# Graph attention in three layers: the last stage run block by block inside layer 2's edge rounds

## The reference, cut to what matters

```
h    = x @ W_lin + b_lin
feat = h @ W_gat                                   # 8 heads of 32
e    = leaky_relu(el[src] + er[dst], 0.2)          # el, er: feat times two vectors
a    = softmax of e over the edges of one dst
out  = sum over edges of feat[src] * a + gat_bias
out  = leaky_relu(out, 0.01)
x    = layernorm(x + h + out)                      # the result
```

## Time and profile before

| | us |
|---|---|
| median of 3 runs | 6509.73 |
| lowest and highest run | 6506.02 and 6517.36 |
| span of the profiled execution | 6515.9 |
| of it from the last product of layer 2 to the end | 154 |

### The profile page before, as it was taken

The page is one execution under the profiler, slowest core; times in us unless marked ns, Lnnn a source line. Parts: engine busy times, 40 slices in busy tenths (PEclk is TensorE's granted clock), DMA queues, the critical chain, the costliest instruction groups (busy, mean ns, idle before and its releaser), DMA issues. The chain is left out here.

```text
span 6515.9 us, 110173 instructions
## 1 busy us (share of the span) xinstructions
PE 4981.0 (76%) x21652; PEld 3682.0 (57%) x21653; DVE 5313.4 (82%) x16735; ACT 2717.7 (42%) x4351; POOL 4585.1 (70%) x4837
## 2 busy tenths in 40 slices
PE   6788888888888577777777777758778778787876
PEld 5555655555556355555555555536656556566653
DVE  6788888888888788888888888877778778777788
ACT  3333333333333245554545455533333333333335
POOL 2777777777776577776767676737777777777764
PEclk8777877877777678777777777767777777778786
DMA  8555555555555455555555555535555555555545
GB/s 274 149 156 156 157 157 155 157 156 156 156 155 141 117 162 160 160 159 156 159 158 162 153 162 157 162 102 161 160 158 161 160 159 161 160 160 160 160 131 159
DMA packets 505894, 1027.11 MB, mean 158 GB/s; under 512 B 146891, under 2 KB 313199, under 8 KB 504878
## 3 DMA queue, kind: packets, MB, share of 16 engines
q0 software_dynamic: 226208, 633.50, 36.2%
q1 hardware_dynamic: 278798, 382.44, 18.1%
HBM read 931.37 MB, written 84.15 MB: 156 GB/s over the span
## 5 line engine op out<-in xcount | busy, mean ns | idle before, releaser
L1032 POOL DMA_INDIRECT e_rows<-table,loaded x4689 | 4489.2, 957 | 1756.8 <-issue 1392.6
L1266 PE MATMUL e_p_mm<-e_rows,e_onehot 128*128 128x264 f32 x9378 | 2466.5, 417 | 0.0
L1266 PEld LDWEIGHTS e_p_mm<-e_rows,e_onehot 128*128 128x128 f32 x9378 | 1876.3, 208 | 360.5 <-issue 20.1
L1444 DVE TENSOR_TENSOR e_rows<-e_rows,e_p_pair 128x1024 f32<-128x1024 f32 x1173 | 1417.8, 1209 | 0.0
L1436 DVE TENSOR_TENSOR e_onehot<-e_col,e_p_pair 128x512 f32<-128x512 f32 (+1 forms) x1467 | 953.4, 650 | 328.2 <-issue 280.4
L1259 PE MATMUL e_p_mm<-e_xmsg,e_onehot 128*128 128x264 f32 x1764 | 875.3, 669 | 103.3 <-ACT e_p_mm L1133 86.2
L1274 PE MATMUL e_p_one<-ad_parts,e_onehotT 128*128 x5586 | 707.8, 188 | 149.6 <-issue 143.3
L1225 ACT ACTIVATE e_rows<-e_gap 128x64 f32<-128x64 f32 (+1 forms) x294 | 80.6, 274 | 1621.0 <-DVE e_gap L1766 1614.7
L1274 PEld LDWEIGHTS e_p_one<-ad_parts,e_onehotT 128*128 128x128 bf16 x5586 | 550.4, 102 | 330.4 <-issue 193.3
L1139 ACT ACTIVATE e_onehotT<-e_onehotT,minus_pidx 128x2432 bf16<-128x2432 bf16 x294 | 681.0, 2316 | 42.0 <-DMA e_pass<-pass_rows 42.0
L1142 ACT ACTIVATE e_onehotT<-e_onehotT,one_col 128x2432 bf16<-128x2432 bf16 x294 | 682.6, 2322 | 9.6
(11 more groups left out here) (326 smaller groups left out, 5819.3 us busy)
## 6 DMA issues: line engine op xcount, KB each, us to landing
e_onehotT<-rel_rows SPq DMA_DIRECT2D x294, 608.0 KB
e_rows<-table,loaded POOLq DMA_INDIRECT x4689
e_own_row<-table SPq DMA_DIRECT2D x196, 128.0 KB
table<-e_rows_out SPq DMA_DIRECT2D x98, 132.0 KB
table<-n_rows_out SPq DMA_DIRECT2D x14, 910.0 KB, 15.6
table<-e_rows_out SPq DMA_DIRECT2D x98, 130.0 KB
n_inputs<-in_x_turned SPq DMA_DIRECT2D x14, 896.0 KB, 11.2
e_mask<-mask_rows SPq DMA_DIRECT2D x196, 64.0 KB
```

Of the source, the lines that this page charges most:

```text
L1032: pool.indirect_dma_start(rows[k][:, g, 0:TW], None, table[L], bass.IndirectOffsetOnAxis(ap=idx[k][:, g:g + 1], axis=0)).then_inc(s_gat[k] ...
L1266: ins = nc.tensor.matmul(p_mm[:, bass.ds(region, MW)], onehot[:, g, :], rows[k][:, g, :], start=False, stop=True, skip_group_check=True)
L1444: return nc.vector.tensor_tensor(feats, feats, p_e[:, gs, :].unsqueeze(3).to_broadcast([P, n, H, C]), ALU.mult)
```

## The change

`final_phase`, the array `resid` and `add_linear` are gone. In their place layer 2's rounds call `last_blocks` on SP and VectorE, `last_sums` on TensorE, and `inverse_roots`, `above_zero` and `last_rows` on ScalarE. Round w makes the share of place w - 4, the sums of place w - 5 and the scaled rows of place w - 6, and SP stores place w - 9 in its own round w. `summed` and `mv` have two buffers, `vin` and `turned` one. The two sums of a block, one for the part above zero and one with the residual and the slope 0.01, stand in the two halves of one PSUM bank. The inverse root is exp(-0.5 ln(var + eps)). After the last round the loops go on to drain the last blocks. Layer 2 now writes out 12 rounds, and no semaphores are cleared behind it.

```diff
 # SP, in round w, ahead of its wait for the look-up of round w - 2
+def last_blocks(w, u, i):
+    r, other = u % TURNS, (u + 1) % TURNS
+    if finished(w, 6):
+        if finished(w, 7):
+            wait_apart(sp, s["mm"], place_of(sp, w, 7))
+        sp.dma_start(turned[:].rearrange("p k e -> p (k e)"),
+                     turned_dram[bass.ds(place_of(sp, w, 7), 1)].rearrange("o p e -> (o p) e")).then_inc(s_rst[r], 16)
+    if finished(w, 9):
+        natural, = words(sp, WINDOW_ROW, ..., 1, NODES_PAD - P)
+        wait_apart(sp, s["node"], place_of(sp, w, 9))
+        sp.dma_start(t["out"][bass.ds(natural, P), :], summed[other][:]).then_inc(s_out[other], 16)
-        store_summed(w - 2, ago(2))
-        load_turned(w - 1)
 # ScalarE
+def above_zero(w, u, i):
+    r = (u - 5) % TURNS
+    act.wait_ge(s["mm"], place_of(act, w, 5))
+    if finished(w, 7):
+        act.wait_ge(s_out[r], count(act, pair_of(u, i, 7) * 16))
+    nc.scalar.activation(summed[r][:], p_node[:, 0:D], ACT.Relu, scale=1.0 - OUT_SLOPE).then_inc(s["part"], 1)
+def inverse_roots(j, r):
+    act.wait_ge(s["mean"], j)
+    nc.scalar.activation(root[:, r:r + 1], mv[:, r, 1:2], ACT.Ln, bias=eps_col[:, 0:1]).then_inc(s["root"], 1)
+    act.wait_ge(s["root"], j)
+    nc.scalar.activation(rinv[:, r:r + 1], root[:, r:r + 1], ACT.Exp, scale=-0.5).then_inc(s["rinv"], 1)
+def last_rows(w, u, i):
+    act.wait_ge(s["shift"], place_of(act, w, 6))
+    nc.scalar.activation(summed[r][:], summed[r][:], ACT.Identity, bias=shift[:, r:r + 1], scale=rinv[:, r:r + 1]
+                         ).then_inc(s["node"], 1)
 # ScalarE, body: after the columns, ahead of lookup_rows and clear_sums
-        act.wait_ge(st["linear"], now)
-        if not first:
-            act.wait_ge(s_linout, count(act, w * 16))
-        nc.scalar.copy(summed[:], p_node[:, 0:D]).then_inc(st["kept"], 1)
+    if LINEAR and finished(w, 6):
+        inverse_roots(place_of(act, w, 6), (u - 6) % TURNS)
+    if LINEAR and finished(w, 5):
+        above_zero(w, u, i)
 # ScalarE, body: after clear_sums
+    elif finished(w, 6):
+        last_rows(w, u, i)
 # TensorE, body: right after the transposed scores
+def last_sums(w, u, i):
+    r = (u - 5) % TURNS
+    wait_apart(pe, s["v1"], place_of(pe, w, 5))
+    if finished(w, 6):
+        wait_apart(pe, s["value"], place_of(pe, w, 6))
+    nc.tensor.matmul(p_node[:, 0:D], one_parts, bias2_parts, start=True, stop=False)
+    nc.tensor.matmul(p_node[:, 0:D], ident[:], vin[:], start=False, stop=True)
+    pe.wait_ge(s_rst[r], count(pe, pair_of(u, i, 5) * 16))
+    nc.tensor.matmul(p_node[:, D:2 * D], one_parts, lin_parts, start=True, stop=False)
+    for c in range(2):
+        nc.tensor.matmul(p_node[:, D:2 * D], turned[:, c, :], lin[:, c, :], start=False, stop=False)
+    nc.tensor.matmul(p_node[:, D:2 * D], slope_ident, vin[:], start=False, stop=True).then_inc(s["mm"], 1)
 # VectorE, body: last_blocks after the fourth quarter, ahead of extras; last_shift after the first quarter
+def last_blocks(w, u, i):
+    ...                    # add the two halves (part, then value), every third round safe sums and reciprocals
+    ...                    # bn_stats, bn_aggr
+    if finished(w, 4):
+        dve.wait_ge(s["att"], count(dve, group_of(u, i, 4)))
+        if finished(w, 5):
+            wait_apart(dve, s["mm"], place_of(dve, w, 5))
+        nc.vector.tensor_tensor(vin[:]..., num, share[...], ALU.mult).then_inc(s["v1"], 1)
-    final_phase()
```

More of the change, by code:

```diff
@@ L682, in _ @@
                         last.then_inc(s["fold"], 1)
[L684 to L815, removed]
-                    nc.vector.scalar_tensor_tensor(buf(value, b)[:], buf(y, b)[:, 0:D], OUT_SLOPE, buf(part, b)[:], ALU.mult, ALU.add
-                                                   ).then_inc(s["value"], 1)
-                def statistics(b):
-                    dve.wait_ge(s["value"], b + 1)
-                    nc.vector.bn_stats(buf(stats, b)[:], buf(value, b)[:]).then_inc(s["stats"], 1)
-                def mean(b):
-                    dve.wait_ge(s["stats"], b + 1)
-                    nc.vector.bn_aggr(mv[:, b, :], buf(stats, b)[:]).then_inc(s["mean"], 1)
-                def inverses(c):
-                    first, n = spans[c]
-                    dve.wait_ge(s["root"], c + 1)
-                    nc.vector.reciprocal(rinv[:, first:first + n], root[:, first:first + n]).then_inc(s["rinv"], 1)
-                def shifts(c):
-                    first, n = spans[c]
-                    dve.wait_ge(s["rinv"], c + 1)
-                    nc.vector.scalar_tensor_tensor(shift[:, first:first + n], mv[:, first:first + n, 0], -1.0,
-                                                   rinv[:, first:first + n], ALU.mult, ALU.mult).then_inc(s["shift"], 1)
-                safe_sums(0)
-                shares(0)
-                for i in range(BLOCKS + SHIFT + 1):
-                    if i - SHIFT in end_of:
-                        shifts(end_of.index(i - SHIFT))
-                    if i - RINV in end_of:
-                        inverses(end_of.index(i - RINV))
-                    if 0 <= i - MEAN < BLOCKS:
-                        mean(i - MEAN)
-                    if 0 <= i - STATS < BLOCKS:
-                        statistics(i - STATS)
-                    if 0 <= i - SUM < BLOCKS:
-                        value_sum(i - SUM)
-                    if i < BLOCKS:
-                        value_share(i)
-                    j, at = divmod(i, SHARES)
-                    if at == SHARES - 8 and (j + 1) * SHARES < BLOCKS:
-                        safe_sums(j + 1)
-                    if at == SHARES - 6 and (j + 1) * SHARES < BLOCKS:
-                        shares(j + 1)
@@ L862, in build_program @@
               "gap", "expo", "erow", "first_y", "first_l", "first_d", "fdist", "fmat", "factor", "rescaled",
-              "msg0", "msg1", "msg2", "msg3", "settled", "added", "square", "extras", "cols", "cleared", "linear", "kept")
+              "msg0", "msg1", "msg2", "msg3", "settled", "added", "square", "extras", "cols", "cleared")
     st = {n: sem("e_" + n) for n in STAGES}
@@ L871, in build_program @@
     s_apart = sem("e_apart")
-    s_lin, s_turned, s_linout = (sem(f"e_{n}") for n in ("lin", "turned", "linear_out"))
+    s_lin = sem("e_lin")
     def edge_phase(L):
@@ L926, in edge_phase @@
                 turned = sbuf(ph, tag + "turned", [P, 2, P], F32)
-                summed = sbuf(ph, tag + "summed", [P, D], F32)
-                lin_parts, one_parts = (sbuf(ph, tag + n, [2 * 32 + 1, w], BF16)[:] for n, w in (("lin_parts", D), ("one_parts", P)))
+                lin_parts, bias2_parts, one_parts = (sbuf(ph, tag + n, [2 * 32 + 1, w], BF16)[:]
+                                                     for n, w in (("lin_parts", D), ("bias2_parts", D), ("one_parts", P)))
                 lin = sbuf(ph, tag + "lin", [P, 2, D], F32)
+                slope_ident = as32[:, 0:P]
+                share, safe = (sbuf(ph, tag + n, [P, BUFS, H], F32) for n in ("share", "safe"))
+                vin = sbuf(ph, tag + "vin", [P, D], F32)
+                summed = [sbuf(ph, f"{tag}summed{r}", [P, D], F32) for r in range(TURNS)]
+                stats, mv = sbuf(ph, tag + "stats", [P, 6], F32), sbuf(ph, tag + "mv", [P, TURNS, 2], F32)
+                root, rinv, shift = (sbuf(ph, tag + n, [P, TURNS], F32) for n in ("root", "rinv", "shift"))
             adst, l1, l2, gap = (sbuf(ph, tag + n, [P, G, H], F32) for n in ("adst", "l1", "l2", "gap"))
@@ L1095, in body @@
                         sp.dma_start(loaded[k][:], col_dram[:, bass.ds(w * COL_W, COL_W)]).then_inc(s_idx[L][k], 16)
[L1096 to L1098 removed]
                     if CARRY:
                         carried(w, u, i)
+                    else:
+                        last_blocks(w, u, i)
                     wait_apart(sp, st["lookup"], ago(TURNS))
@@ L1238, in _ @@
                 clear_sums(W0 + WINDOWS)
-                if not CARRY:
-                    merge_exponentials()
-                for w in range(WINDOWS, BLOCKS + 8) if CARRY else ():
+                for w in range(WINDOWS, BLOCKS + 8 if CARRY else BLOCKS + 7):
                     u, i = w % UNROLL, w // UNROLL
@@ L1244, in _ @@
                         merge_exponentials()
+                    if LINEAR:
+                        inverse_roots(w - 6, (u - 6) % TURNS)
+                        if finished(w, 5):
+                            above_zero(w, u, i)
+                        last_rows(w, u, i)
+                        continue
                     if NORMED and finished(w, 6):
@@ L1412, in _ @@
                     last.then_inc(s["turned"], 1)
+                    for w in range(WINDOWS + 1, BLOCKS + 6):
+                        last_sums(w, w % UNROLL, w // UNROLL)
             @block.vector
@@ L1671, in body, with last_shift @@
+                def last_shift(w, u):
+                    r = (u - 6) % TURNS
+                    dve.wait_ge(s["rinv"], place_of(dve, w, 6))
```

(9 more changed lines are left out.)

85 lines of the change are left out of this document (54 added, 31 removed).

## The result

The change makes the kernel slower: 6805.38 us, median of 4 runs (6801.97 to 6814.37), against 6508.19 for the kernel before (median of 4; the 6509.73 of the table above is that of the first 3); the ratio is 1.0454, 95% interval 1.0441 to 1.0466. The forecast was 6764.

What follows compares the result with a forecast made beforehand. GpSimd's gather issue bounds rounds at 20.28 us, TensorE's loop through ScalarE only just as short. Rounds +326, jumps +31, last stage -103 gave +254 on 6515.9: 6770, less the 6.2 offset 6764; range 6610 to 6920.

Steps and rivals of the forecast that it cites:

- SP's part of the delay: On SP, from the sums' end to the store's issue: wake-up 0.26, load issue 0.36, word load 0.5, gaps 0.35 us.
- The landing: Time from the issue of SP's result store to its landing: 1.9 us, from 1.7 to 3.9.
- D: Delay from the sums' end on TensorE to ScalarE's start, through SP's store: 3.5 us, bounds 3.0 and 6.3.
- TensorE's sums: Five matmuls become ten, adding 1.35 us; sums end 3.0 after the transpose, bounds 2.2 and 3.6.
- The round: Layer 2's round becomes 23.9 us, 3.6 above 20.28; rounds 8 to 97 pay it, 326 in all.
- The jump back: The loop's jump costs 2.2 us with nothing making it up: 14 passes, 31 us, bounds 0 and 60.
- The drain: Places 94 to 98 after the last products: five times 8.4 us; with merge and end 51 replaces 154, so -103.
- VectorE: Added work of 1.9 us on 16.0 a round fits the longer round and adds nothing on the path.
- Ln and Exp hidden: On ScalarE ahead of the Relu, some 0.29 us each, hidden in waiting time, as would be a table load.
- Rival (1): Store landed before the sums are ready; rounds 20.5 us, 120 saved behind the last products, total 6408; chance 0.07.
- Rival (2): ScalarE's wait remains, but full-clock sums of 2.2 and D of 3.0 give rounds of 22.3 us, total 6586; chance 0.09.
- Rival (3): Stores land at 3.9 us behind the load and among gathers; D 5.5, rounds 27.6, total 7106; chance 0.06.

Runs made afterwards that it cites:

- shorter-delay kernel: Changed kernel with SP reading the word before its wait for the sums, then issuing the store ahead of the turned block's load: 6630.38 us.
- written-out kernel: Changed kernel with layer 2's rounds all written out, no loop and no jump back: 6758.79 us.
- store-first kernel: Changed kernel with SP reading the word and issuing the result's store before it waits for the sums: 6454.82 us, ratio 0.9921 to the kernel before.
- kernel with both repairs: Changed kernel with SP's store ahead of its wait for the sums and ScalarE's Relu behind one-hot passes and clearing: 6400.56 us, ratio 0.9829 to the kernel before.

## Why the prediction was right, point by point

The mechanism was right, and the experiments show it rather than argue it: the wait sits where the prediction put it (for 95 of 98 blocks: the 90 rounds and five of the drain), it goes one for one into the round, and taking it away at either end brings back the old pace.

- *SP's part of the delay.* Sums to store 1.39 against 1.47 forecast. SP's word load took 0.44 (0.5 forecast).
- *The landing* was undersized: 2.7, not 1.9, so D is 4.2 as a median and not 3.5. The row of 1.9 was taken in a stage where no gathers ran. A load of 128 KB stood some 0.6 ahead of most stores there too: with one, up to 6491, they landed in 2.0 as a median, and those from then on, with no loads left to issue, in 1.7:

```profile
DMA to landing us min/median/max: 1.7/2.0/3.9
```

```profile
DMA to landing us min/median/max: 1.7/1.7/1.9
```

In the drain the load is issued 0.90 ahead of the store, and with the gathers over the store lands in 1.72 (above, at 6758.43):

```profile
6757.53 0.34 SPq L879 DMA_DIRECT2D e_turned<-turned  x1
```

In the rounds, beside the gathers, the same load costs the store 0.8, as the shorter-delay kernel shows. So neither the load nor the gathers did it alone here; how the two together delay a store was not tested.
- *TensorE's sums* were oversized: 2.23 after the transpose, not 3.0. They start 0.11 after it and not 0.46 as in the earlier trace rows; and the five more matmuls, four 4-byte ones and a 2-byte one, add 0.91 (2.12 from first to last in place of 1.21), not 1.35. In the round shown what follows a 4-byte one starts 0.22 after it, and what follows a 2-byte one 0.11. The forecast's 0.27 was the length of L1312's row over four, which counts the end of the last one in. The clock is no part of it: it was full in the round shown, and full already in that of the earlier trace rows. So the prediction's bound of 2.2, put there for a stretch at full clock, was met for another reason, which is luck. First the kernel before, then the changed one:

```profile
5418.80:5420.50 1.70, 1.52 (x6) 0.88 (x6) 1.36 (x5) 0.00 (x0) 1.16 (x2) 1.00 0.31 85
```

```profile
5836.27:5842.63 6.36, 4.90 (x33) 3.49 (x31) 5.83 (x19) 0.00 (x0) 5.02 (x5) 1.00 0.52 139
```

- *The round.* The two errors, +0.7 and -0.8, cancel: a median of 23.9 to 24.0 against 23.9, so 326 for 90 rounds stands; that it stands to the tenth is luck.
- *The jump back* is the term that failed in size. It said 14 passes of 2.2, with nothing to make it up: 31, bounds 0 and 60. Measured: the 13 passes with a jump take 1930.8, 148.5 each, against 143.4 for six rounds of 23.9: 66, which is 35 more than forecast and above the upper bound (14 passes jump back 13 times). The stall itself is near what was forecast (2.56); what was missed is what follows it, half a clock for the sums of the next round and a store that starts later for it. Of the distance of 34 between the forecast span, 6770, and the measured one the rounds make 33 (389.8 against 326 + 31) and the later start of layer 2 makes 4 (3.8, where under 1 was forecast); what comes behind the last round gives 2 back (-105.2 against -103). The 3.8 may be chance: the written-out kernel began layer 2 another 7.6 later, with the same code ahead of it. The rest of the 41 up to 6805 is the offset: the profiled execution of before lay 6.2 above its median, that of after 1.1 below. So the 6.2 was no fixed distance between profile and time, and carrying it into the forecast was a mistake of 7.
- *The drain.* From the last products to the end 49.5 against 51; -104.6 against -103 (the earlier trace rows for before). From the sums of one of its five blocks to those of the next it took 7.4, 9.1, 13.4 (with the merge, 4.3, in it) and 9.7, where 8.4 was forecast (the one shown is the 7.4, from the first 4-byte matmul at 6755.59 to the next one at 6762.95). Here too errors cancel: the store landed in 1.72, so D was 2.8 and not 3.5, and behind the pauses of the drain the sums took 3.65 and not 2.7, at a granted clock of 0.50 (6762.95 to 6766.60).
- *VectorE.* 699.35 / 40.3 = 17.4 a round, +1.4 where +1.9 was forecast, and nothing on the path.
- *Ln and Exp hidden, the table too:* right, and stronger than said; even two loads in every round stay hidden.
- *Rival (1)*, the store landed already, is what the store-first kernel makes true: 20.47 a round against the 20.5 worked out there (the sums shorter, the stretch from the extra tiles longer, which cancels once more), 121 saved behind the last round against 120, and a span of 6449 against 6414, the difference being the jumps (3.4 a pass in 10 passes). *Rival (2)*'s 2.2 for the sums came true, though not by a change of clock, and its short landing did not. *Rival (3)*'s late landing came only in single rounds.

## What to carry to other kernels

When a stage is folded into a pipelined loop, list for each buffer who frees it and what the freeing instruction itself waits for; if that is an event of the same round as the wait, the whole way of the transfer lies on the path, however many buffers there seem to be. Issue what frees a buffer ahead of the waits that it doesn't need, and put an instruction that may wait behind those on which others depend; either was worth 350 to 395 us of 6800 here, for a few moved lines. And price a stall by what it leaves behind: a pause of 2.56 on TensorE cost 5 us when no slack stood behind it.

## What the runs showed of the hardware

- A store of 128 KB that was issued about 1 us behind a load of 128 KB landed in 1.72 us in the drain, where no gathers ran, and in 2.7 as the median of 49 stores of the changed kernel, most of them in rounds, beside gathers; in one round 4.6 passed from its issue to the start of the waiting engine. With the load put behind it this time was 1.93, in place of 2.74. In the rounds of the kernel with both repairs, where SP issues the edges' masks (128 KB) some 3 us and their columns (33.5 KB) some 1 us ahead of the store, it landed in 3.2 as the median of the 43 stores that the trace resolves, and nobody waited for it:

```profile
DMA to landing us min/median/max: 1.7/3.2/4.7
```

- TensorE's granted clock behind a pause was not the lower, the longer the pause. In the first 4.3 us behind it, it was 0.60 after 2.56 us of standing still at the jump (above), and after the wait of 5.62 in the round shown, the 3.75 of the shorter-delay kernel and the 1.52 of the store-first kernel it was 0.50, 0.58 and 0.50, the lower level of 1.2 GHz or near it:

```profile
5848.81:5853.11 4.30, 4.30 (x10) 3.28 (x11) 1.07 (x7) 0.24 (x1) 2.11 (x3) 0.50 0.38 109
```

```profile
5629.22:5633.52 4.30, 4.30 (x12) 3.37 (x13) 1.76 (x9) 0.23 (x1) 3.39 (x4) 0.58 0.42 110
```

```profile
5308.37:5312.67 4.30, 4.30 (x10) 3.24 (x11) 4.00 (x14) 0.24 (x1) 3.38 (x4) 0.50 0.64 203
```

- A table load on ScalarE costs 1.28 us of the engine and, in a kernel where ScalarE waits for others, nothing of the time: two in each of some 80 rounds left 6400.31 against 6400.56.
